# Transposing attention outputs by DMA instead of TensorE, with three PSUM banks taking turns

## The reference

```python
# layer 1: x = x + attention(layernorm(x))
qkv = inputs @ W_qkv                       # 256 -> 32 q heads, 16 k heads, 16 v heads of 64
k = jnp.repeat(k, 2, axis=1); v = jnp.repeat(v, 2, axis=1)   # two q heads share one k, v head
scores = jnp.einsum('bhqd,bhkd->bhqk', q, k) / math.sqrt(HEAD_DIM) + bias[None]   # ALiBi
scores = jnp.where(causal[None, None], scores, -jnp.inf)
out = jnp.einsum('bhqk,bhkd->bhqd', jax.nn.softmax(scores, axis=-1), v)
out.transpose(0, 2, 1, 3).reshape(B, S, Q_DIM) @ W_out
# layer 2: x = x + ffn(layernorm(x)), low rank 64
P = x @ U1; H = jax.nn.gelu(P @ V1 + b1); Q = H @ U2; return Q @ V2 + b2
```

## Time and profile before

| | |
|---|---|
| median of 3 runs | 3042.26 us (3040.5 to 3043.39) |
| profiled execution, its own time | 3041.37 us |
| span of its trace | 3039.6 us |
| TensorE busy, share of the span | 2813.3 us, 93% |
| VectorE | 2194.7 us, 72% |
| ScalarE | 2190.9 us, 72% |
| GpSimd | 1730.0 us, 57% |
| DMA queue of Sync | 188.32 MB, 26.3% of 16 engines |

### The profile page before, as it was taken

The page is one execution under the profiler, slowest core; times in us unless marked ns, Lnnn a source line. Parts: engine busy times, 40 slices in busy tenths (PEclk is TensorE's granted clock), DMA queues, the critical chain, the costliest instruction groups (busy, mean ns, idle before and its releaser), DMA issues.

```text
span 3039.6 us, 99681 instructions
## 1 busy us (share of the span) xinstructions
PE 2813.3 (93%) x32328; PEld 1966.0 (65%) x32328; DVE 2194.7 (72%) x6987; ACT 2190.9 (72%) x3892; POOL 1730.0 (57%) x1560
## 2 busy tenths in 40 slices
PE   4999999999989999999999999999899999999986
PEld 1666675766757666676666767667676666767664
DVE  6777677776767777677776777767677776777763
ACT  3767777777777777777777777777777777776783
POOL 1555565555655656555565665556555555565664
PEclk9999999999999999999999999999999999999998
DMA  5332232322223222232322323222232322323210
GB/s 169 68 72 58 63 71 46 79 58 69 62 55 77 53 72 60 56 76 49 78 58 60 73 47 79 55 72 60 56 75 50 77 59 56 73 48 82 55 35 8
DMA packets 220087, 195.25 MB, mean 64 GB/s; under 512 B 41738, under 2 KB 217866, under 8 KB 219274
## 3 DMA queue, kind: packets, MB, share of 16 engines
q1 hardware_dynamic: 219540, 188.32, 26.3%
HBM read 27.73 MB, written 8.39 MB: 12 GB/s over the span
## 4 chain that ended last, share of the span: by engine, by line
PE 31%; issue 27%; POOL 27%; ACT 5%; DVE 3%; POOLq 1%; ACTq 0%; DVEq 0%
POOL p_lo L1090 26%; PE proj L445 13%; PE scores L445 7%; PE o_acc L445 6%; PE max_scores L445 2%; PE ffn_acc L445 2%; ACT h_f L824 1%; ACT L738 1%; DVE v_lo L851 1%; ACT p_f L738 1%; ACT L824 1%; POOL h_lo L1113 1%; PE transposes L567 1%; DVE max_scores L925 1%; POOLq L327 1%
## 5 line engine op out<-in xcount | busy, mean ns | idle before, releaser
L1090 POOL TENSOR_TENSOR p_lo<-p_f,p_hi 128x512 f16<-128x512 f32 x1280 | 1476.6, 1158 | 1073.3 <-ACT p_hi L696 1070.8
L738 ACT ACTIVATE p_f<-scores 128x512 f32<-128x512 f32 x1280 | 756.4, 591 | 333.9 <-PE scores L445 211.5
L696 ACT ACTIVATE p_hi<-p_f 128x512 f16<-128x512 f32 x1280 | 802.3, 627 | 48.0 <-issue 33.7
L925 DVE CUSTOM_DVE_ANT_0 max_scores<-max_scores,causal 128x384 f32<-128x384 f32 (+3 forms) x1184 | 564.1, 508 | 274.6 <-PE max_scores L445 265.3
L445 PE MATMUL scores<-q_hi_lo,k_lo_hi 128*128 128x512 f16 (+3 forms) x2048 | 613.1, 300 | 28.4 <-issue 28.0
L445 PE MATMUL scores<-q_hi_aug,k_hi_aug 128*128 128x512 f16 (+3 forms) x2048 | 585.7, 299 | 0.0
L445 PE MATMUL o_acc<-v_hi_one,p_lo 128*128 128x65 f16 x5120 | 517.6, 194 | 13.7 <-POOL p_lo L1090 13.7
L445 PE MATMUL o_acc<-v_hi_one,p_hi 128*128 128x65 f16 x5120 | 517.9, 194 | 0.0
L445 PE MATMUL o_acc<-v_lo,p_hi 128*128 128x64 f16 x5120 | 517.7, 193 | 0.0
L445 PEld LDWEIGHTS o_acc<-v_hi_one,p_lo 128*128 128x128 f16 x5120 | 471.7, 98 | 49.7 <-issue 12.8
L445 PEld LDWEIGHTS o_acc<-v_lo,p_hi 128*128 128x128 f16 x5120 | 468.4, 98 | 19.5
(11 more groups left out here) (115 smaller groups left out, 5205.9 us busy)
## 6 DMA issues: line engine op xcount, KB each, us to landing
q_hi_aug<-q_pair_hi SPq DMA_DIRECT2D x512, 64.0 KB, 2.0
q_hi_lo<-q_pair_hi SPq DMA_DIRECT2D x512, 64.0 KB, 2.1
q_hi_lo<-q_pair_lo SPq DMA_DIRECT2D x512, 64.0 KB, 2.0
k_hi_aug<-k_pair_hi SPq DMA_DIRECT2D x256, 64.0 KB, 2.0
k_lo_hi<-k_pair_hi SPq DMA_DIRECT2D x256, 64.0 KB, 2.0
k_lo_hi<-k_pair_lo SPq DMA_DIRECT2D x256, 64.0 KB, 2.2
x_rows<-in_L_attn_inputs SPq DMA_DIRECT2D x17, 512.0 KB, 3.7
x_residual<-in_L_attn_inputs SPq DMA_DIRECT2D x16, 512.0 KB, 3.7
```

The source lines that it names most:

```text
L696: return nc.scalar.activation(out_ap, in_ap, ACT.Copy, scale=scale)
L738: nc.scalar.activation(p_f[:, k % 3, :], score_bank[k % 2][:, :], ACT.Exp).then_inc(exp_done, 1)
L925: last = nc.vector.tensor_tensor_reduce(out=bank, in0=bank, in1=causal[:, (T - 1 - qt) * P:S], scale=1.0, scalar=-3e38, op0=ALU.add, op1=A ...
L1090: nc.gpsimd.tensor_tensor(p_lo[:, slot, n, :], p_f[:, k % 3, :], p_hi[:, slot, n, :], ALU.subtract).then_inc(lo_p, 1)
```

## The change

`transpose_o`, its bank and the VectorE instruction for `o_t_lo` go. Instead, ScalarE copies `o_f` (now two buffers) to fp16 in segment 4 of the same step as attend, GpSimd subtracts to get the low half (both in the new tile `o_hi_lo`, two slots), and Sync issues one DMA transpose per head, 128 x 1024 fp16 in eight blocks of 128 x 128, into the ring `o_t`, which now holds both halves. `project_out` waits for the transposes' semaphores `ot_in` and moves from segment 3 to segment 4; with it moves all that VectorE does in `OUT_SEG`, the statistics of the second layer norm included. The bank that the transposes had joins the proj banks, so that projections, x, ln2 and max transposes take turns over three. `x_residual` goes; Sync loads x directly into `x_acc`, one token tile of 128 KB in each of steps 10 to 13 instead of 512 KB in step 2.

```diff
-MAX_SEG, K_SEG, V_SEG = 1, 0, 4
-
-OUT_RING, OUT_GROUP, OUT_LAG, OUT_SEG = 8, 4, 12, 3
+MAX_SEG, K_SEG, V_SEG, O_SEG = 1, 0, 4, 4
+
+OUT_RING, OUT_GROUP, OUT_LAG, OUT_SEG = 8, 4, 12, 4
...
+            if (s, n) in X_PAIRS:
+                uses.append(("x", X_PAIRS[s, n]))
...
+            if (s, n) in LN2_T_AT:
+                uses.append(("ln2", LN2_T_AT[s, n]))
...
-PROJ = {use: k % 2 for k, use in enumerate(projection_order())}
+BANKS = 3
+PROJ = {use: k % BANKS for k, use in enumerate(projection_order())}
...
-        o_f = sb("o_f32", [P, T, 2 * HD], F32)
+        o_f = sb("o_f32", [P, 2, T, 2 * HD], F32)
+        o_hl = sb("o_hi_lo", [P, 2, 2, S], F16)
-        ot = [sb(f"o_t_{p}", [P, OUT_RING, S], F16) for p in ("hi", "lo")]
+        ot = sb("o_t", [P, OUT_RING, 2, S], F16)
-        xres = sb("x_residual", [P, T, D], F32)
-        proj_bank = [psum("proj0"), psum("proj1")]
-        t_bank = psum("transposes")
+        proj_bank = [psum(f"proj{b}") for b in range(BANKS)]
...
 # Sync, at the end of step s
-                    if s == 2 and mode != LAST:
-
-                        if 16 * i - OUT_LAG > 0:
-                            sp.wait_ge(acc_done, at(16 * i - OUT_LAG))
-                        sp.dma_start(xres[:, :, :], x_src(i.value())).then_inc(xres_in, 16)
+                    if in_stage(mode, s, ATT + 1):
+                        slot, kv = s % 2, (s - ATT - 1) % KV
+                        sp.wait_ge(lo_o, at(g - ATT))
+                        sp.sem_inc(gate, 1)
+                        sp.dma_start_transpose(ot[:, kv % OUT_RING, :, :].rearrange("p a (t q) -> p (a t) q", q=P),
+                                               o_hl[:, slot, :, :].rearrange("p a q -> p (a q)")).then_inc(ot_in[slot], 16)
+                    if s in range(OUT_LAG - 2, OUT_LAG + 2) and mode != LAST:
+                        t = s - (OUT_LAG - 2)
+
+                        if 16 * i + t - 3 > 0:
+                            sp.wait_ge(acc_done, at(16 * i + t - 3))
+                        sp.dma_start(xacc[:, t, :], x_src(i.value())[:, t, :]).then_inc(xres_in[t], 16)
...
 # TensorE
-                        if n == out_segment(s) and in_stage(mode, s, ATT + 2):
-                            transpose_o(s)
...
-                        pe.wait_ge(lo_ot, at(16 * i + s - OUT_LAG + OUT_GROUP))
+                        for slot in range(2):
+                            pe.wait_ge(ot_in[slot], at(16 * (8 * i + (s - OUT_LAG) // 2 + 2)))
...
 # ScalarE
-                        if n == out_segment(s) and in_stage(mode, s, ATT + 2):
-                            a = g - ATT - 2
-                            act.wait_ge(pe_ot, at(a + 1))
-                            if a_slot(s) % OUT_GROUP == 0:
+                        if n == O_SEG and in_stage(mode, s, ATT + 1):
+                            a, slot = g - ATT - 1, s % 2
+                            landed = 16 * (8 * i + (s - ATT - 1) // 2)
+                            if landed > 0:
+                                act.wait_ge(ot_in[slot], at(landed))
+                            if s % OUT_GROUP == 0:
 
                                 if out_before(i, s) > 0:
                                     act.wait_ge(pe_op, at(out_before(i, s)))
-                            copy(ot[0][:, a_slot(s) % OUT_RING, :], t_bank[:, :]).then_inc(hi_ot, 1)
+                            act.wait_ge(o_done, at(2 * (a + 1)))
+                            copy(o_hl[:, slot, 0, :], o_f[:, slot, :, :].rearrange("p t c -> p (t c)")).then_inc(hi_o, 1)
...
 # VectorE
-                        if n == out_segment(s) + out_lag(s) and in_stage(mode, s, ATT + 2):
-                            dve.wait_ge(hi_ot, at(g - ATT - 1))
-                            low(ot[1][:, a_slot(s) % OUT_RING, :], t_bank[:, :], ot[0][:, a_slot(s) % OUT_RING, :],
-                                1.0).then_inc(lo_ot, 1)
...
 # GpSimd
+                        if n == 0 and in_stage(mode, s, ATT + 2):
+                            slot = (s - ATT - 2) % 2
+                            pool.wait_ge(hi_o, at(i * KV + s - ATT - 1))
+                            nc.gpsimd.tensor_tensor(o_hl[:, slot, 1, :], o_f[:, slot, :, :].rearrange("p t c -> p (t c)"),
+                                                    o_hl[:, slot, 0, :], ALU.subtract).then_inc(lo_o, 1)
```

More of the change, by code:

```diff
@@ L148, in projection_order, with last_uses @@
     return uses
-PROJ = {use: k % 2 for k, use in enumerate(projection_order())}
-MULTIPLES = (1, 2, 4, 8, 16, 32, 64, 80, 192)
+BANKS = 3
+PROJ = {use: k % BANKS for k, use in enumerate(projection_order())}
+FFN_USES = ("ln2", "p", "h", "y")
+def last_uses(b):
+    mine = [use for use in projection_order() if PROJ[use] == b]
+    steady = [use for use in mine if use[0] not in FFN_USES]
+    return {mine[-1], steady[-1]}
+MULTIPLES = (1, 2, 4, 8, 16, 32, 64, 80, 128, 192)
 FREE = 1
@@ L560, in attend @@
                     last.then_inc(pe_av, 1)
-                def transpose_o(s):
-                    a = i * KV + s - ATT - 2
-                    bank = transposes_bank(lo_ot, a + 1)
-                    pe.wait_ge(o_done, at(2 * (a + 1)))
-                    for qt in range(T):
-                        last = nc.tensor.transpose(bank[:, qt * P:(qt + 1) * P], o_f[:, qt, :], ident[:, :])
-                    last.then_inc(pe_ot, 1)
                 def project(bank, col, semaphore):
@@ L598, in transpose_x2 @@
                     u = (i - 1) * 4 + t
[L599 removed]
+                    bank = next_proj(("ln2", t))
                     pe.wait_ge(x2n_done, at(u + 1))
```

102 lines of the change are left out of this document (51 added, 51 removed).

## The result

The changed kernel takes 3001.69 us (median of 4 runs, 2999.87 to 3005.82) against 3042.82 of the kernel before on the same chip: a ratio of 0.9861, 95% interval 0.9849 to 0.9873. It is 1.4% faster, where 4.1% was forecast (2917 us): the direction is right and the time lies in the wide range of 2850 to 3160 us, but not in the forecast's own of 2850 to 2965 us, and the gain is a third of what was said.

The account below looks back on a forecast made before the run. TensorE's instruction stream was taken as the bound, except in the feed-forward steps, where ScalarE sets the pace. The sum was 3041.4 - 99 - 40 - 15 + 15 + 15 = 2917 us, own range 2850 to 2965, wide range 2850 to 3160.

Parts of the forecast that it names:

- Removed transposes, -99 us: On TensorE, four fp32 transposes per kv head go, 0.44 us a set, counted in 224 of 256 steps: 99 us off.
- Third bank, -40 us: TensorE's waits for a bank's last reader shrink with three banks in turns: 40 us off, between 0 and 64.
- The move of the output projection: From segment 3 to 4: no change in TensorE's counts; later second-layer-norm statistics delay GpSimd, 15 us added.
- rstd chain: In steps 8 to 11 GpSimd's rstd waits for VectorE's statistics, with subtraction and last p_lo queued behind: 15 us added.
- What covers the new subtraction: On GpSimd before attend, about 4.6 us of cover against 4.1 us of ScalarE instructions and two subtractions.
- VectorE's relief, -15 us: Without o_t_lo, 0.69 us less per step on VectorE shrinks TensorE's 48.8 us of waits before max_scores: 15 us off.
- GpSimd in the feed-forward steps, +15 us: In two steps per batch h_lo work may leave the new subtraction uncovered: 15 us added, 37 at most.
- The DMA transpose, price 0: On Sync's queue, 2.4 us of hold per transpose, landing some 4 us after the start, costs TensorE nothing: 0 us.
- T: How long one DMA transpose holds Sync: taken as 2.4 us, TensorE seeing nothing up to 3.8 us.
- the low bound: DMA transpose cut into the rows of its eight blocks, 1024 pieces of 256 B: 3.7 us on 16 engines.
- Rival 1: TensorE's freed time is lost waiting for the exp chain on ScalarE and GpSimd: 3009 us, 2965 to 3060, chance 0.20.
- Rival 2: Sync's queue becomes the bound because the transpose holds it, from 3.9 us per transpose: 4007 us, chance 0.24.

Follow-up runs that it names:

- the fastest kernel: Changed kernel, projection in segment 3 in steps 13 to 15, first variance and both GpSimd rstds moved, attention-output subtraction on VectorE: 2921.25 us, ratio 0.9592.
- two edits: Changed kernel with the projection in segment 3 in step 15 alone, first variance at (7, 3), second normalisation's rstd in the next step's segment 0: 2937.61 us, 0.9642.
- the runs with a later subtraction: GpSimd's last p_lo put ahead of the subtraction: with the projection in segment 3 everywhere 3098.19 us; with step 15's projection and GpSimd's small operations moved 3011.70 us.
- The two runs with this edit before it: Subtraction on VectorE: with the projection in segment 3 everywhere 3022.66 us; with segment 3 in steps 13 to 15 and GpSimd's small operations early 2928.23 us.

## Why the prediction was right and wrong

- **Removed transposes, -99 us.** 2.8%, 85 us, in the setting of the whole change, three banks and segment 4. Part of this agreement is luck: the 85 us are net of the new subtraction and hold what the ring of banks gains by one use less, and in the other settings the same exchange saves 37 us (three banks, segment 3) or costs 37 (two banks, segment 3) or 12 (two banks, segment 4). It isn't a price of the operation.
- **Third bank, -40 us.** Mis-sized, and not one number either: with DMA transposes it gains 129 us in segment 4 and 66 in segment 3; with TensorE's transposes it gains 32 in segment 4 and loses 8 in segment 3. The waits in the earlier trace rows didn't show it, because they belong to an order of uses that the change takes apart.
- **The move of the output projection** is the step that failed: "changes no count on TensorE", with 15 us for the rstd chain as its only price. The loop's end, missing altogether, measured 36 us, 30 of them by y1's bank alone. GpSimd's order measured 32 us. Its mechanism was right for the second layer norm; the wait for the first variance, which I had overlooked, was there before the change, and the subtraction made it dear. I had counted TensorE's instructions at the loop's end and not asked which bank the last of them takes and what stands behind it, a branch. Together 68 us where 15 stood in the sum: 53 of the 85 us that the forecast was too low.
- **What covers the new subtraction** was mis-sized too: 4.6 us of cover against 4.1 of work was taken for enough outside the feed-forward steps. With the projection in segment 3 it isn't, and the waits for p_lo are 85.5 us against 13.7. So putting the projection back doesn't win the 53 us back but costs 13; in the loop it is even.
- **VectorE's relief, -15 us.** It did not come: the waits for row_max rose from 48.8 to 82.2 us although VectorE has 200.9 us less to do. That TensorE now arrives earlier at the same chain is my reading; no run tests it. In the fastest kernel they are 61.2.
- **GpSimd in the feed-forward steps, +15 us.** Not seen: step 13 is 0.54 us shorter. Step 14 is 0.93 us longer, its segment 4 with the projection 2.30 instead of 1.15; but with the projection back in segment 3 in these steps alone step 14 gains 0.15 us only, and three banks beside TensorE's transposes lengthen it by 1.2 us without any subtraction. What lengthens it is open. The subtraction's own 1156 ns are as forecast, 1158.
- **The DMA transpose, price 0.** Right in the change itself: T = 1.255 us where 2.4 was taken, landed in 3.1 against 4, TensorE's waits for o_t and k_lo_hi 3.6 and 5.3 us. The extra packets are 271104 / 256 = 1059 per transpose, near the low bound's 1024 pieces of 256 B. The Trainium skill's figure, in "VectorE: DVE Perf Modes", section "The three transpose paths", of 1309 ns for one 128x128 block doesn't add up block by block here: eight blocks land in 3.1 us. The Trainium skill's page "Advanced Engine Details and Errata", section "X-Bar Transpose (TRN2)", by which transposing DMAs are as fast as regular ones, was the better guide: the 3.1 us for 256 KB lie between 2.0 us for a 64 KB copy and 3.9 for a 512 KB load.
- **The rivals.** Rival 1 named the time well (3009 us), by luck, and one of its signs, waits for p_lo, is there (44.8 us). But the freed time was not lost to the exponentials' own pace, as it held: two edits that leave the exponentials and their three buffers as they are bring 2937 us. Rival 2 did not happen, but the runs with a later subtraction show that it was near: 0.9 and 1.3 us more of Sync's wait per transpose cost 81 and 74 us.
- **The sum.** With the two places mended the kernel takes 2937.6 us. Without the 15 us for them the forecast would be 2902, so some 35 us of it did not come; of these VectorE's relief is 15, and how the rest divides is open, since the parts don't add. The fastest kernel's 2921 us are near the forecast's 2917, but they needed two further edits and don't confirm it.

## What to carry over

When a change moves an instruction, look at three things besides its duration: which buffer every later use in the turns gets (four uses of three banks in the last segment cost 30 us, by a wait shortly before a branch that shows as 0.03 us in the stream), which small operation of a slow engine waits for its result with what queued behind it, and which chain it used to cover or covers now. Savings from parts that share a ring of buffers can't be added: here each of three parts cost time alone, and together they gained 1.4%. Compare the loop and what lies around it apart before blaming a mechanism in the loop: the kernel with the projection back in segment 3 is slower only outside the loop. And in a queue that works in order, a wait for a later producer is paid by everything behind it.

## What the runs showed of the hardware

- A DMA transpose of 128 x 1024 fp16 values between places in SBUF holds the issuing queue for 1.255 us and lands in 3.1 us (medians of 256), against 2.0 us for a 64 KB copy and 3.9 for a 512 KB load in the same trace.
- What VectorE's subtraction with both inputs in SBUF takes depends on what GpSimd is doing when it starts. In the fastest kernel no GpSimd instruction was running at the start of 133 of the 256, and these took 0.68 to 0.69 us each, also the 117 beside which GpSimd's p_lo started later. The other 123 started while p_lo was running, and 110 of them took over 0.9 us, up to 1.66: where p_lo had more than 0.15 us to go (121), they ended 0.547 us after it (0.544 to 0.551). The two runs with this edit before it show the same 0.547. Shortest, median and longest in ns:
```profile
L969 DVE TENSOR_TENSOR o_hi_lo<-o_f,o_hi_lo x256: 679/693/1656, 94.4 to 2867.4; 128x512 f16<-128x512 f32 x128
```
- TensorE's 14 gaps over the loop's branch are 1.65 to 2.35 us before the change and 2.94 to 4.92 after it, where a wait for a bank stands shortly before the branch; with that wait gone they are 1.91 to 2.53 us. The granted clock can be lower behind them, and the gap's length alone doesn't tell when: over the next 12 us it was 1.00 in all 14 cases before the change, 0.74 to 0.88 in all 14 after it, and 0.86 in ten of the 14 with y1 in the other bank.
